# Moving the next head pair's query product to the end of two attention steps, and its cast on ScalarE behind another cast

## Chip, cores and metric

One Trainium2 chip, one of its cores. The metric is the device time of one execution in microseconds (us), lower is better. A profiled execution comes with its own time, its span (first to last instruction on the engines) and a trace of every instruction.

## What is computed

A block of three parts on x of shape 2 x 512 x 256 in float32: half a mixture-of-experts layer, causal attention with 16 heads of size 128 over a latent of size 64, and the same half layer again. Cut to what matters:

```python
x = x + 0.5 * ffn(layernorm(x))        # 12 experts, top 2, capacity 1.25
latents = x @ W_down.T                 # layernormed x; latent size 64
keys, values = latents @ W_uk.T, latents @ W_uv.T
q = x @ W_q.T                          # 16 heads of 128
scores = q @ keys.T / sqrt(128)        # causal, 512 x 512 for each head and sequence
x = x + (softmax(scores) @ values) @ W_o.T
x = x + 0.5 * ffn(layernorm(x))
```

## The kernel before

The weights of queries and keys are folded into one matrix (`Mq`), so that a head's queries live in the latent space and scores are products of queries (`uc`) with the latents (`latT_hi`, `latT_lo`). Values and output weights are folded in the same way (`Nv`), and are applied after the attention (line 1212). Every number is carried as a high and a low 16-bit part, so most products stand two or three times, and each result is read out of a PSUM bank twice: ScalarE (ACT) casts the high part, then VectorE (DVE) subtracts it and writes the low part.

The attention runs over 8 pairs of heads, `i`, and in each over 10 units of work, `j`; five units cover one head for both sequences. Each engine has its own program, in which `attention_step(i, j)` stands for j = 1 to 10 in a loop over the first 7 pairs (lines 1203, 585, 857) and once more, unrolled, for the last pair. Engines meet only at semaphores. In step j:

- TensorE (PE) makes the **scores** of unit j+4 (lines 1129 to 1131, the last one adds the mask), the **context** of unit j (lines 1152 to 1154) and the **transposes** of the probabilities of unit j+2 (line 1139). The context needs the low part of the transposed probabilities (`pTlo_ready`), the transposes need the exponentials.
- ACT makes the **exponentials** of unit j+3 (line 550) when their row maximum is there, and the **high part** of the transposed probabilities of unit j+2 (line 556).
- DVE makes the **low part** of unit j+1 (line 803), which needs ACT's high part, and the **row maximum** of unit j+4 (lines 794, 798), which needs the scores. In steps 3, 5, 8 and 10 it first copies a finished context out (lines 811, 812).
- GpSimd (POOL) divides the copied contexts (lines 415 to 421); the sync engine's queue (SP) moves queries and transposes contexts (lines 317, 309).

In steps 1 and 3 the **queries** of the next pair come in between, for the first and the second half of the tokens (`queries(i + 1, 0)`, `queries(i + 1, 1)`): PE makes them in six matmuls of 512 columns into bank 7 (line 900), ACT casts the high part (line 542), DVE subtracts (line 785), which is its last work in these steps, and SP then issues four transfers from `stage` to `uc` for each half (line 317). The scores of the next pair's unit 0 (made in step 6) wait for the first half's transfers, those of its unit 2 (made in step 8) for the second half's. Bank 7 also holds scores: those of unit 9, made in step 5, wait until both halves of the queries have been read.

Of the kernel before, what the change touches and what calls it, by code (L numbers as in the profile page):

```python
# [5 lines left out]
def bass_macaron_moe_mla_moe(  # L6
# [72 lines left out]
    with ctx:  # L79
# [196 lines left out]
        def tokens(t):  # L276
            return slice(t * HALF, (t + 1) * HALF)

        def blk(n):
            return slice(n * P, (n + 1) * P)  # L280

        def beyond(i, j):

            return isinstance(i, int) and i * UNITS + j >= NP * UNITS
# [146 lines left out]
        def _(act):  # L431
# [105 lines left out]
            def split_queries(i, t):  # L537

                if not isinstance(i, int):
                    act.wait_ge(u_moved[t], i * 64)  # L540
                act.wait_ge(u_ps, i * 2 + (t + 1))
                nc.scalar.copy(stage[:, 0, tokens(t)], bank[2 * t if isinstance(i, int) and i == 0 else 7][:, :]).then_inc(u_hi, 1)

            def exponent(i, j):

                u = j % UNITS
                act.wait_ge(max_ready, i * UNITS + (j + 1))
                for n, (b, q, at) in enumerate(HEAD_UNITS[u % HU]):
                    cols = slice(at, at + P * (q + 1))
                    last = nc.scalar.activation(prob[:, u % 2, cols], bank[SCORE_BANK[u]][:, cols], ACT.Exp,  # L550
                                                bias=nmax[:, u, n:n + 1])
                last.then_inc(prob_ready, 1)

            def split(i, j):
                act.wait_ge(pT_ps, i * UNITS + (j + 1))
                nc.scalar.copy(pT_hi[:, j % 2, :], bank[3 + j % 2][:, :]).then_inc(pThi_ready, 1)  # L556

            def attention_step(i, j, queries=True):
                if not beyond(i, j + 3):
                    exponent(i, j + 3)  # L560
                if queries and j in (1, 3):
                    split_queries(i + 1, j // 2)
                if not beyond(i, j + 2):
                    split(i, j + 2)

            split_N(0)
            for k in range(DC, 2 * DC):
# [14 lines left out]
            exponent(0, 2)  # L582
            split(0, 1)
            attention_step(0, 0)
            with act.Fori(0, NP - 1) as i:
                for j in range(1, UNITS + 1):
                    attention_step(i, j)
            for j in range(1, UNITS - 2):
                attention_step(NP - 1, j, queries=False)
# [16 lines left out]
        def _(dve):  # L606
# [181 lines left out]
            def row_max(i, j):  # L788
                u = j % UNITS
                dve.wait_ge(s_ps, i * UNITS + (j + 1))  # L790
                parts = HEAD_UNITS[u % HU]
                src = bank[SCORE_BANK[u]]
                if len({q for _, q, _ in parts}) == 1:
                    last = nc.vector.tensor_reduce(nmax[:, u, 0:len(parts)], src[:, :].rearrange("p (a n) -> p a n", a=len(parts)),  # L794
                                                   AX.X, ALU.max, negate=True)
                else:
                    for n, (b, q, at) in enumerate(parts):
                        last = nc.vector.tensor_reduce(nmax[:, u, n:n + 1], src[:, at:at + P * (q + 1)], AX.X, ALU.max, negate=True)  # L798
                last.then_inc(max_ready, 1)
# [93 lines left out]
        def _(pe):  # L893
            mm = nc.tensor.matmul

            def split_product(dst, left, right, K, start=True, stop=True):

                terms = [(0, 0, k) for k in range(K)] + [(0, 1, k) for k in range(K)] + [(1, 0, k) for k in range(K)]
                for n, (a, b, k) in enumerate(terms):
                    last = mm(dst, left(k)[a], right(k)[b], start=start and n == 0, stop=stop and n == len(terms) - 1)  # L900
                return last
# [201 lines left out]
            def queries(i, t):  # L1103

                first = isinstance(i, int) and i == 0
                if not first:
                    pe.wait_ge(u_lo, i * 2 + t)
                split_product(bank[2 * t if first else 7][:, :],
                              lambda k: [m[:, k, bass.ds(i * 2, 2), :].rearrange("p h l -> p (h l)") for m in Mq],
                              lambda k: [xT_hi[:, k, tokens(t)], xT_lo[:, k, tokens(t)]], DC).then_inc(u_ps, 1)  # L1110

            def scores(i, j):
                u = j % UNITS
                first_use = {0: 0, 2: 1}
                if u in first_use:
                    pe.wait_ge(u_moved[first_use[u]], i * 64 + 64 * (j // UNITS + 1))
                if HELD_BY[u] is None:
                    if not (isinstance(i, int) and i == NP - 1):
                        pe.wait_ge(u_lo, i * 2 + 4)
                else:  # L1120
                    held = HELD_BY[u] + j - u
                    if not (isinstance(i, int) and i * UNITS + held < 0):
                        pe.wait_ge(prob_ready, i * UNITS + (held + 1))
                dst = bank[SCORE_BANK[u]]
                for n, (b, q, at) in enumerate(HEAD_UNITS[u % HU]):
                    cols = slice(at, at + P * (q + 1))
                    keys = slice(SEQ * b, SEQ * b + P * (q + 1))
                    queries_of = uc[:, i * 2 + j // HU, SEQ * b + P * q:SEQ * b + P * (q + 1)]
                    mm(dst[:, cols], queries_of, latT_hi[:, keys], start=True, stop=False)  # L1129
                    mm(dst[:, cols], queries_of, latT_lo[:, keys], start=False, stop=False)  # L1130
                    last = mm(dst[:, cols][:, P * q:], identb[:, :], maskneg[:, :], start=False, stop=True)  # L1131
                last.then_inc(s_ps, 1)

            def transposes(i, j):
                pe.wait_ge(prob_ready, i * UNITS + (j + 1))
                if not (isinstance(i, int) and i == 0 and j < 2):
                    pe.wait_ge(pTlo_ready, i * UNITS + (j - 1))
                for k in range(SB):
                    last = nc.tensor.transpose(bank[3 + j % 2][:, blk(k)], prob[:, j % 2, blk(k)], ident[:, :])  # L1139
                last.then_inc(pT_ps, 1)  # L1140

            def context(i, j):
                unit = j % HU
                if unit == 0 or unit == 2:
                    pe.wait_ge(ctx_free, i * (2 * B) + (j // HU * B + unit // 2 + 1))
                pe.wait_ge(pTlo_ready, i * UNITS + (j + 1))
                for b, q, at in HEAD_UNITS[unit]:
                    dst = bank[5 + b][:, q * (LAT + 1):(q + 1) * (LAT + 1)]
                    for k in range(q + 1):
                        n = SB * b + k  # L1150
                        p_hi, p_lo = (p[:, j % 2, at + P * k:at + P * (k + 1)] for p in (pT_hi, pT_lo))
                        mm(dst, p_hi, lat[:, n, 0:LAT + 1], start=(k == 0), stop=False)  # L1152
                        mm(dst[:, 0:LAT], p_hi, lat[:, n, LAT + 1:2 * LAT + 1], start=False, stop=False)  # L1153
                        last = mm(dst, p_lo, lat[:, n, 0:LAT + 1], start=False, stop=(k == q))  # L1154
                if unit in LAST_UNIT:
                    last.then_inc(ctx_ps, 1)

            def attention_step(i, j, with_queries=True):
                if with_queries and j in (1, 3):
                    queries(i + 1, j // 2)  # L1160
                if not beyond(i, j + 4):
                    scores(i, j + 4)
                context(i, j)
                if not beyond(i, j + 2):
                    transposes(i, j + 2)

            pe.wait_ge(wuv_lo, 1)
            pe.wait_ge(woT_ready, 16 * 2 * DC)
# [31 lines left out]
            pe.wait_ge(lat_ready, 1)  # L1200
            pe.wait_ge(m_lo, 4)
            attention_step(0, 0)
            with pe.Fori(0, NP - 1) as i:
                for j in range(1, UNITS + 1):
                    attention_step(i, j)
# [11 lines left out]
            for j in range(1, UNITS):  # L1217
                attention_step(NP - 1, j, with_queries=False)
# [43 lines left out]
```

## Time and profile before

| what | value |
|---|---|
| median of 3 runs (lowest to highest) | 245.18 us (245.15 to 245.21) |
| profiled execution, its own time | 245.21 us |
| its span | 243.5 us |
| PE busy, share of the span | 231.6 us, 95% |
| DVE busy | 201.6 us, 83% |
| ACT busy | 163.2 us, 67% |
| POOL busy | 79.8 us, 33% |
| granted TensorE clock | 0.999 of full speed |

A row of a timeline gives a start, a duration, the engine, the line in the code and, in brackets, the idle time before it and what ended it. PE's matmuls are pipelined: the next one starts before the modelled end of the last, so the time that a part takes of PE is read from its start to the start of the next part. On DVE, too, an operation can start shortly before the row of the one ahead of it ends.

### The profile page before, as it was taken

To read this page: it belongs to the slowest core of one execution; us is meant where nothing else is said; L and a number is where in the kernel's file an instruction comes from. 1 tells how busy PE (TensorE), PEld (TensorE's weight loads), DVE (VectorE), ACT (ScalarE), POOL (GpSimd) and SP (SyncE) were. 2 spreads that over 40 slices of the span, in tenths; PEclk is the share of its full clock that TensorE was granted. 3 is DMA by queue.
4 is the path that set the end of the run, shared out by engine and by line. 5 is a ranking of instruction groups with operands and counts; after the bars stand their busy time and mean duration, and the time that the engine had idled before them with its cause. 6 is when DMAs were issued, how large, how long until landed. Compare 5 with 4: busy or idle time off the path is not lost.

```text
span 243.5 us, 7145 instructions
## 1 busy us (share of the span) xinstructions
PE 231.6 (95%) x2579; PEld 177.3 (73%) x2604; DVE 201.6 (83%) x480; ACT 163.2 (67%) x316; POOL 79.8 (33%) x135
## 2 busy tenths in 40 slices
PE   7699999899999999999999999999998899999995
PEld 2465479757777788787887787878886788865474
DVE  3978799987899999899999998999998338268793
ACT  2678883547788888879798888897988300344560
POOL 8351865000024344345234343452345000300320
PEclk9999999999999999999999999999999999999999
DMA  6999984002021025142160251331613310000005
GB/s 216 259 382 297 197 153 89 3 23 63 3 53 38 0 75 100 31 93 49 43 129 0 75 97 31 86 56 43 129 28 61 65 24 0 3 0 0 3 1 172
DMA packets 43128, 19.30 MB, mean 79 GB/s; under 512 B 33820, under 2 KB 42856, under 8 KB 42856
## 3 DMA queue, kind: packets, MB, share of 16 engines
q1 hardware_dynamic: 41912, 17.91, 32.0%
q10 hardware_dynamic: 1200, 1.18, 1.4%
q8 instruction: 10, 0.16, 0.3%
q14 instruction: 6, 0.05, 0.1%
HBM read 7.55 MB, written 1.05 MB: 35 GB/s over the span
## 4 chain that ended last, share of the span: by engine, by line
PE 75%; DVE 14%; DMA 4%; issue 3%; ACT 2%; SPq 1%; ACTq 0%; DVEq 0%
PE bank L949 12%; PE bank L1139 11%; PE bank L900 11%; PE bank L1212 9%; PE bank L1130 7%; PE bank L1129 4%; PE bank L1057 3%; PE bank L1153 3%; PE bank L1152 3%; PE bank L1154 3%; DMA cT<-in_L_ffn_w_dram 2%; DVE pT_lo L803 2%; PE bank L1131 2%; DVE nmax L794 2%; PE bank L907 2%
## 5 line engine op out<-in xcount | busy, mean ns | idle before, releaser
L550 ACT ACTIVATE prob<-bank,nmax 128x384 f32<-128x384 f32 (+3 forms) x128 | 62.2, 526 | 8.9 <-DVE nmax L794 7.4
L803 DVE TENSOR_TENSOR pT_lo<-bank,pT_hi 128x512 f16<-128x512 f32 x80 | 54.8, 685 | 3.0 <-ACT pT_hi L556 2.1
L556 ACT CAST pT_hi<-bank 128x512 f16<-128x512 f32 x80 | 46.7, 584 | 11.0 <-PE bank L1139 10.5
L1139 PE MATMUL bank<-ident,prob 128*128 128x128 f32 x320 | 50.5, 280 | 0.0
L415 POOL TENSOR_TENSOR cst<-craw,rsum 128x256 f32<-128x256 f32 x30 | 18.4, 612 | 87.0 <-DVE craw L812 87.0
L1152 PE MATMUL bank<-lat,pT_hi 128*128 128x65 bf16 x320 | 37.7, 193 | 1.9 <-DVE pT_lo L803 1.9
L1153 PE MATMUL bank<-lat,pT_hi 128*128 128x64 bf16 x320 | 37.8, 195 | 0.0
L1130 PE MATMUL bank<-latT_lo,wqo 128*128 128x384 bf16 (+3 forms) x128 | 36.6, 299 | 1.2
L1154 PE MATMUL bank<-lat,pT_lo 128*128 128x65 bf16 x320 | 37.5, 192 | 0.0
L1152 PEld LDWEIGHTS bank<-lat,pT_hi 128*128 128x128 f16 x320 | 30.1, 96 | 6.9 <-DVE pT_lo L803 2.0
L794 DVE TENSOR_REDUCE nmax<-bank 128x1 f32<-128x512 f32 (+1 forms) x48 | 32.8, 683 | 1.9 <-PE bank L1131 1.9
L1139 PEld LDWEIGHTS bank<-ident,prob 128*128 128x128 f32 x320 | 33.6, 140 | 0.0
L1154 PEld LDWEIGHTS bank<-lat,pT_lo 128*128 128x128 f16 x320 | 30.1, 99 | 0.0
L1153 PEld LDWEIGHTS bank<-lat,pT_hi 128*128 128x128 f16 x320 | 30.0, 97 | 0.0
L1129 PE MATMUL bank<-latT_hi,wqo 128*128 128x384 bf16 (+3 forms) x105 | 29.5, 282 | 0.4 <-DMA wqo<-stage 0.4
L1131 PE MATMUL bank<-maskneg,identb 128*128 128x128 bf16 x128 | 26.4, 219 | 0.0
L798 DVE TENSOR_REDUCE nmax<-bank 128x1 f32<-128x384 f32 x64 | 23.9, 416 | 2.0 <-PE bank L1131 2.0
L421 POOL TENSOR_TENSOR ffn_buf<-cst,woT_buf 128x256 f32 (+1 forms) x30 | 20.1, 671 | 4.8 <-POOL woT_buf L419 4.7
L1212 PE MATMUL bank<-Nv_hi,cT 128*128 128x256 bf16 x128 | 21.3, 273 | 0.0
L1212 PE MATMUL bank<-Nv_lo,cT 128*128 128x256 bf16 x64 | 17.4, 273 | 0.0
L1131 PEld LDWEIGHTS bank<-maskneg,identb 128*128 128x128 bf16 x128 | 12.5, 98 | 6.2
L1129 PEld LDWEIGHTS bank<-latT_hi,wqo 128*128 (+1 forms) x128 | 12.5, 98 | 4.6 <-issue 0.7
(168 smaller groups left out, 453.8 us busy)
## 6 DMA issues: line engine op xcount, KB each, us to landing
wqo<-stage SPq DMA_DIRECT2D x64, 64.0 KB, 2.0
wqo<-in_L_attn_W_o_dram SPq DMA_DIRECT2D x2, 1024.0 KB, 6.6
wqo<-in_L_attn_W_q_dram SPq DMA_DIRECT2D x1, 2048.0 KB, 14.3
out_dram<-X SPq DMA_DIRECT2D x8, 128.0 KB, 1.8
X<-in_L_attn_x_dram ACTq DMA_DIRECT2D x1, 512.0 KB, 7.1
cT<-in_L_attn_W_uk_dram SPq DMA_DIRECT2D x1, 512.0 KB, 16.1
cT<-in_L_attn_W_uv_dram SPq DMA_DIRECT2D x1, 512.0 KB, 11.6
cT<-in_L_ffn_w_dram SPq DMA_DIRECT2D x1, 384.0 KB, 4.9
```

The costliest lines, as they stand in the source:

```text
L550: last = nc.scalar.activation(prob[:, u % 2, cols], bank[SCORE_BANK[u]][:, cols], ACT.Exp, bias=nmax[:, u, n:n + 1])
L556: nc.scalar.copy(pT_hi[:, j % 2, :], bank[3 + j % 2][:, :]).then_inc(pThi_ready, 1)
L794: last = nc.vector.tensor_reduce(nmax[:, u, 0:len(parts)], src[:, :].rearrange("p (a n) -> p a n", a=len(parts)), AX.X, ALU.max, negate=True)
L803: nc.vector.tensor_tensor(pT_lo[:, j % 2, :], bank[3 + j % 2][:, :], pT_hi[:, j % 2, :], ALU.subtract).then_inc(pTlo_ready, 1)
L1129: mm(dst[:, cols], queries_of, latT_hi[:, keys], start=True, stop=False)
L1130: mm(dst[:, cols], queries_of, latT_lo[:, keys], start=False, stop=False)
L1131: last = mm(dst[:, cols][:, P * q:], identb[:, :], maskneg[:, :], start=False, stop=True)
L1139: last = nc.tensor.transpose(bank[3 + j % 2][:, blk(k)], prob[:, j % 2, blk(k)], ident[:, :])
L1152: mm(dst, p_hi, lat[:, n, 0:LAT + 1], start=(k == 0), stop=False)
L1153: mm(dst[:, 0:LAT], p_hi, lat[:, n, LAT + 1:2 * LAT + 1], start=False, stop=False)
L1154: last = mm(dst, p_lo, lat[:, n, 0:LAT + 1], start=False, stop=(k == q))
L1212: last = mm(bank[OUT_BANK[n]][:, 0:D], cT[:, i, part, n, :], Nv[w][:, i, :], start=(i == 0 and (part, w) == TERMS[0]), stop=(i == NP - 1 a ...
```

## The change

Two programs are reordered. On PE the queries of steps 1 and 3 move from the front of the step to its end, behind the transposes. On ACT the cast of the queries moves behind the high part of the transposed probabilities. Nothing is added or removed, and DVE, POOL and SP keep their order.

```diff
@@ ACT @@
             def attention_step(i, j, queries=True):
                 if not beyond(i, j + 3):
                     exponent(i, j + 3)
+                if not beyond(i, j + 2):
+                    split(i, j + 2)
                 if queries and j in (1, 3):
                     split_queries(i + 1, j // 2)
-                if not beyond(i, j + 2):
-                    split(i, j + 2)
@@ PE @@
             def attention_step(i, j, with_queries=True):
-                if with_queries and j in (1, 3):
-                    queries(i + 1, j // 2)
                 if not beyond(i, j + 4):
                     scores(i, j + 4)
                 context(i, j)
                 if not beyond(i, j + 2):
                     transposes(i, j + 2)
+                if with_queries and j in (1, 3):
+                    queries(i + 1, j // 2)
```

On PE, at the end of step 1 in the loop (1139 are the transposes, 900 the queries, 1129 to 1131 the scores of the next step), there stood before:

```order
 L1154 MATMUL bank<-lat,pT_lo 128x65
 L1135 REGISTER_ALU
 L1139 MATMUL bank<-ident,prob 128x128 x4
 L1129 ISA
 L1129 MATMUL bank<-latT_hi,wqo 128x512
 L1130 MATMUL bank<-latT_lo,wqo 128x512
 L1131 MATMUL bank<-maskneg,identb 128x128
```

and there stands now:

```order
 L1154 MATMUL bank<-lat,pT_lo 128x65
 L1135 REGISTER_ALU
 L1139 MATMUL bank<-ident,prob 128x128 x4
 L1107 ISA
 L900 ISA
 L900 MATMUL bank<-xT_hi,Mq_hi 128x512
 L900 ISA
 L900 MATMUL bank<-xT_hi,Mq_hi 128x512
 L900 MATMUL bank<-xT_lo,Mq_hi 128x512 x2
```

The six query matmuls, which stood ahead of step 1's scores, now stand between its transposes and the scores of step 2; step 3 changes in the same way.

On ACT, step 1 in the loop (550 is the exponential, 556 the high part of the transposed probabilities, 542 the cast of the queries):

```order
 L585 ISA
 L550 ACTIVATE prob<-bank0,nmax 128x512
+L555 REGISTER_ALU
+L556 CAST pT_hi<-bank4 128x512
 L540 ISA
 L541 ISA
 L542 CAST stage<-bank7 128x512
-L555 REGISTER_ALU
-L556 CAST pT_hi<-bank4 128x512
 L547 REGISTER_ALU
 L550 ACTIVATE prob<-bank1,nmax 128x384
```

The high part of unit 3 has moved ahead of the cast of the queries.

## Rows read from the trace of the kernel before

**Rows 1.** Busy time of each engine in the first and the seventh pair, from queries to queries.

```profile
core 0: us, PE busy (x) PEld busy (x) DVE busy (x) ACT busy (x) POOL busy (x), PEclk, DMA share, GB/s
64.20:81.03 16.83, 16.23 (x220) 13.07 (x221) 15.64 (x35) 14.12 (x30) 5.11 (x10) 1.00 0.14 34
162.21:178.44 16.23, 16.07 (x220) 13.22 (x222) 15.45 (x36) 13.84 (x29) 6.72 (x12) 1.00 0.30 65
```

**Rows 2.** Timeline of DVE in the seventh pair, steps 1 to 4 and the end.

```profile
162.15 0.68 DVE L803 TENSOR_TENSOR pT_lo<-bank,pT_hi 128x512 f16<-128x512 f32 x1
162.75 0.68 DVE L794 TENSOR_REDUCE nmax<-bank 128x1 f32<-128x512 f32 x1
164.27 0.76 DVE L798 TENSOR_REDUCE nmax<-bank 128x1 f32<-128x384 f32 x2 [0.25 <-PE bank L1131]
...
168.89 0.68 DVE L785 TENSOR_TENSOR stage<-bank,stage 128x512 bf16<-128x512 f32 x1
169.73 0.69 DVE L803 TENSOR_TENSOR pT_lo<-bank,pT_hi 128x512 f16<-128x512 f32 x1 [0.16 <-ACT pT_hi L556]
...
178.38 0.68 DVE L803 TENSOR_TENSOR pT_lo<-bank,pT_hi 128x512 f16<-128x512 f32 x1
```

**Rows 3.** Timeline of PE: queries and scores, then context, transposes and scores of the last pair.

```profile
113.54 0.60 PE L900 MATMUL bank<-xT_hi,Mq_hi 128*128 128x512 f16 x2
114.84 0.33 PE L1129 MATMUL bank<-latT_hi,wqo 128*128 128x384 bf16 x1
115.39 0.19 PE L1152 MATMUL bank<-lat,pT_hi 128*128 128x65 bf16 x1
...
167.53 0.27 PE L1129 MATMUL bank<-latT_hi,wqo 128*128 128x256 bf16 x1
...
179.12 0.20 PE L1152 MATMUL bank<-lat,pT_hi 128*128 128x65 bf16 x1
179.50 0.64 PE L1139 MATMUL bank<-ident,prob 128*128 128x128 f32 x4
179.97 0.38 PE L1129 MATMUL bank<-latT_hi,wqo 128*128 128x512 bf16 x1
180.46 0.19 PE L1152 MATMUL bank<-lat,pT_hi 128*128 128x65 bf16 x1
```

**Rows 4.** Timeline: a query product followed by PE's next scores, ACT's cast, DVE's subtraction.

```profile
118.84 0.27 PE L1129 MATMUL bank<-latT_hi,wqo 128*128 128x256 bf16 x1
119.05 0.58 ACT L542 CAST stage<-bank 128x512 bf16<-128x512 f32 x1
50.96 0.59 ACT L542 CAST stage<-bank 128x512 bf16<-128x512 f32 x1 [0.70 <-PE bank L900]
51.58 0.69 DVE L785 TENSOR_TENSOR stage<-bank,stage 128x512 bf16<-128x512 f32 x1
```

**Rows 5.** First pair: timeline and chain of waits; last line: all 64 transfers.

```profile
64.00 0.69 DVE L803 TENSOR_TENSOR pT_lo<-bank,pT_hi 128x512 f16<-128x512 f32 x1
70.86 0.69 DVE stage L785
73.35 3.44 DMA wqo<-stage
76.92 0.28 PE L1129 MATMUL bank<-latT_hi,wqo 128*128 128x256 bf16 x1 [0.45 <-DMA wqo<-stage]
DMA to landing us min/median/max: 1.9/2.0/3.4
```

**Rows 6.** Timeline of PE and DVE at the end of the attention, where PE waits.

```profile
185.34 0.68 DVE L803 TENSOR_TENSOR pT_lo<-bank,pT_hi 128x512 f16<-128x512 f32 x1
186.08 0.20 PE L1152 MATMUL bank<-lat,pT_hi 128*128 128x65 bf16 x1 [0.52 <-DVE pT_lo L803]
186.54 0.68 DVE L803 TENSOR_TENSOR pT_lo<-bank,pT_hi 128x512 f16<-128x512 f32 x1
187.37 0.19 PE L1152 MATMUL bank<-lat,pT_hi 128*128 128x65 bf16 x1 [0.28 <-DVE pT_lo L803]
```

## The prediction

> **What bounds the kernel now.** I read first the busy times cut by pair of heads [rows 1], because the change acts once in each of the 7 pairs of the loop. The reader is to see that a pair takes 16.23 us (the 7th stands there; the 5th and the 6th take the same), that PE is busy for 16.07 us of it, and that DVE is not far behind with 15.45 us. So PE sets the time, and DVE has only 16.23 - 15.45 = 0.78 us to lose in a pair.
>
> Then I read DVE in order of time [rows 2]. Operations of 512 columns that wait for nothing start 0.60 us apart (162.15, 162.75). DVE rests in steps 1 and 3 only, while PE is at the queries: 0.25 us before the row maximum in step 1, and 0.16 us, among others, behind the subtraction of step 3. From the low part at 169.73 to the end of the one at 178.38 + 0.68 = 179.06 it does not rest at all. In steps 4 to 10 the two engines run at nearly the same pace, and the queries are where DVE catches up.
>
> Last I read how the work is handed over. PE's parts [rows 3]: queries 114.84 - 113.54 = 1.30 us; scores 115.39 - 114.84 = 0.55 us (0.49 us with one piece of 512, 179.97 to 180.46); a context 179.50 - 179.12 = 0.38 us; transposes 179.97 - 179.50 = 0.47 us. ACT's cast of the queries can start 0.21 us after PE's next part (118.84, 119.05), takes 0.58 us, and DVE's subtraction follows 0.03 us later (51.58 against 50.96 + 0.59) [rows 4]. A context that waits starts 0.06 us after the end of its low part (185.34 + 0.68 = 186.02, 186.08) [rows 6].
>
> **The change, part by part.** No instruction is added, removed or made longer; waits move. Before, PE starts the queries at the front of step 1, while DVE still has the low part 1, a row maximum, the low part 2 and another row maximum ahead of it; when DVE comes to the subtraction, the cast is done. Now the queries stand behind context 1 and transposes 3, and context 1 itself waits for low part 1. DVE's program is unchanged, so the subtraction still stands ahead of low part 3, and whatever it waits for holds up low part 3, and so context 3.
>
> Count from the start of context 1, at 0. PE: context 0.38, transposes 0.47, queries 1.30, so 2.15. Cast: 2.15 + 0.21 = 2.36 to 2.94; subtraction at 2.97. DVE had finished low part 1 at -0.06, and the next three operations, 0.60 us apart and the last 0.76 long, end at about 1.82: it stands idle for 1.15 us. Low part 3 starts 0.60 us behind the subtraction and ends 0.69 later, at 4.26; context 3 can start at 4.32. PE, free since 2.15, has scores 6 (0.49), context 2 (0.38), transposes 4 (0.47) and scores 7 (0.55) to do, and is ready at 4.04: it waits 0.28 us. ACT's high part 3 starts when the transposes have landed, some 0.2 us into the queries, and takes 0.58 us of their 1.30, so it does not delay the cast behind it: that edit costs nothing. If it were not there, the cast of the queries would hold up high part 3, since the transposes now end first.
>
> Step 3 repeats this: from context 3 again 2.97 us to the second subtraction, at 7.29. DVE has a context copy more to do there and rests less. Behind the second subtraction DVE works without a gap: 0.60 us to low part 5, then 9.33 us (169.73 to 179.06) to the end of low part 11, which is the next pair's low part 1, and 0.06 us to its context [rows 2, 6]. That is 7.29 + 0.60 + 9.33 + 0.06 = **17.28 us**, and this chain closes on itself, so no pair behind another can be shorter. Does something else end later? PE alone needs from the end of the second queries (6.46) what it needs now from 167.53 to 178.44, where the pair ends, less step 3's own three parts: 10.91 - 1.40 = 9.51, and 0.55 for the scores ahead of the context: 16.5, or 16.7 with the 0.17 us for which scores 9 would wait for bank 7. Not longer. So the pair grows from 16.23 to 17.28 us, by 1.05 us, and DVE rests for 17.28 - 15.45 = 1.8 us of it in place of 0.78.
>
> The transfers are the one thing late next. Scores 12 in step 8 wait for the four transfers of the second half: the fourth is issued 73.35 - 70.86 = 2.49 us after the subtraction starts, lands 2.0 us later by the median, and the scores start 0.13 us behind (76.79, 76.92) [rows 5]. From there to the end of the pair are 81.03 - 76.92 = 4.11 us [rows 1, 5], and 0.55 for scores to the next context 1. In total 7.29 + 2.49 + 2.0 + 0.13 + 4.66 = 16.57 us, 0.71 us less than the chain through DVE: hidden. In the first pair that same transfer took 3.44 us, and PE waited for it [rows 5]. With 3.44 us the chain is 18.01 us and sets the first pair. I take the 3.44 us there, because it is the row of the very transfer concerned, and 2.0 us in the other six.
>
> On this the Trainium skill, "DMA: Bandwidth & Descriptors", section on the fixed cost of a transfer, has a rule: about 2.0 us plus the bytes at 436 GB/s. For the 64 KB here that is an estimate of 2.15 us, and with it the first pair would be 17.28 us too, and the time 251.8 us. The median of 2.0 us agrees with it, the first pair's 3.44 us does not.
>
> **The sum.** In the first pair, step 1 begins at 64.20, now with the queries; changed, with scores, and context 1 starts at 64.20 + 0.55 = 64.75 (low part 1 ends at 64.69) [rows 1, 5]. The next pair's comes 18.01 us later, at 82.76, and six more pairs of 17.28 us lead to 186.44. In the trace the last pair's context 1 starts at 179.12, and there too it has waited for its low part (179.06) [rows 2, 3]; no queries follow, so from there on all is as before. The attention ends 186.44 - 179.12 = 7.3 us later. The profiled execution took 245.21 us, 0.03 above the median of the runs, so the forecast is **252.5 us**, against 245.18. With 2.0 us for the transfer it is 251.8. If a waiting context starts 0.15 us behind its low part, as one does (187.22, 187.37) [rows 6], two such hand-overs in each of 7 pairs add 7 x 2 x 0.09 = 1.3 us: 253.8. If part of the chain overlaps better than I count, by 0.3 us in a pair, it is 2.1 us less, and 249.8 at the shorter transfer.
>
> **The rivals.** A difference under 0.2%, some 0.5 us, can hardly be told from no change here.
> - *DVE catches up* and only the 0.28 us at context 3 stay in each pair, 7 x 0.28 = 2 us: 247.2. For it: PE and DVE are nearly even. Against it: DVE has no gap from 169.73 to 179.06 in which to catch up, and its 15.45 us of work and 1.8 us of rest do not fit into 16.5. Chance 0.05.
> - *PE stays busy throughout*: if DVE enters step 1 early enough that context 1 need not wait, the stall falls into PE's own work: 245.2. Against it: low part 1 ends at 162.15 + 0.68 = 162.83, and without the queries ahead of it context 1 would be wanted at 162.22 + 0.55 = 162.77 [rows 1, 2]; DVE is late already. Chance 0.05.
> - *Faster*: a wait of PE goes. In step 8 of the first pair PE stands 0.45 us before scores 12 for the transfer of 3.44 us [rows 5], and that pair takes 16.83 us where a later one takes 16.23 [rows 1]. If the transfer is met at its usual 2.0 us, it lands 1.44 us sooner; so long as the second subtraction comes less than 1.44 us later against PE's own work, and PE's work covers every other wait, the 0.6 us are gain: 244.6. Against it: the later pairs would have to stall nowhere. Chance 0.04, half of it beyond 0.2%.
> - *The transfers set every pair*: if all of them take 3.44 us as in the first pair, 18.01 us in seven pairs, 6 x 0.73 = 4.4 us more: 256.9. Against it: the median over 64 is 2.0 us. Chance 0.03.
>
> **How the numbers follow.** The forecast has a chance of 0.83, and its own bounds, 249.8 to 253.8 with a little room above for hand-overs that I did not see, are the range: 249.8 to 254.1; the four rivals lie outside and hold 0.17. Slower: 0.83 + 0.05 + 0.03 = 0.91. Same: 0.05 and half of the third rival, 0.07. Faster: 0.02.
>
> **What would show it.** In the changed profile a pair (queries to queries) should take about 17.3 us from the second on; DVE should rest ahead of line 785, some 1.15 us in step 1 and less in step 3, released by ACT's line 542; PE should wait at line 1152 for DVE's line 803, at first by about 0.3 us; ACT's line 542 should wait for PE's line 900; PE's busy time should stay and DVE's too. The prediction is wrong if pairs still take 16.23 us, if DVE rests ahead of line 785 without PE waiting behind it, or if PE's waits end on transfers.

## The result, and the profile after

The changed kernel takes 252.07 us (median of 4, 252.02 to 252.4) against 245.17 us before (244.72 to 245.21): ratio 1.028, 95% interval 1.0258 to 1.0302. It is slower by 6.9 us; 252.5 was forecast. The profiled execution took 252.04 us with a span of 250.3, so the whole loss lies in the span (243.5 before).

The busy times by engine from the profile's page of the changed kernel: no engine has more work. DVE's 200.9 us were 201.6 before, ACT's 162.2 were 163.2. PE shows 235.7 in place of 231.6 with the same number of matmuls, and the groups of matmuls sum to the same (line 1139 to 50.5 us before and after, line 1130 to 36.6). What differs is when they start: the page counts time in which two matmuls overlap once, so matmuls that waits have pulled apart make more busy time.

```profile
PE 235.7 (94%) x2579; PEld 176.1 (70%) x2604; DVE 200.9 (80%) x480; ACT 162.2 (65%) x316; POOL 79.8 (32%) x135
```

The groups of instructions from the same page. The last column is the idle time ahead of a group:

```profile
L550 ACT ACTIVATE prob<-bank,nmax 128x384 f32<-128x384 f32 (+3 forms) x128 | 62.2, 526 | 17.4 <-DVE nmax L794 11.9
L556 ACT CAST pT_hi<-bank 128x512 f16<-128x512 f32 x80 | 46.6, 583 | 1.7 <-PE bank L1139 1.1
L785 DVE TENSOR_TENSOR stage<-bank,stage 128x512 bf16<-128x512 f32 x16 | 11.1, 692 | 14.6 <-ACT stage L542 14.6
```

Line 785, the subtraction of the queries, waited for the cast once before, for 0.7 us in the whole kernel; now DVE stands 14.6 us ahead of it. Cut by pair, from one first subtraction to the next, the first pair and two later ones (these answer to [rows 1]):

```profile
67.79:85.45 17.66, 16.70 (x223) 13.01 (x223) 15.35 (x35) 13.78 (x29) 6.72 (x12) 1.00 0.13 32
102.69:119.93 17.24, 16.66 (x223) 12.98 (x223) 15.26 (x35) 13.71 (x29) 6.72 (x12) 1.00 0.28 61
119.93:137.18 17.25, 16.67 (x223) 12.97 (x223) 15.26 (x35) 13.71 (x29) 6.72 (x12) 1.00 0.28 61
```

A pair takes 17.24 us in place of 16.23, with DVE working 15.26 us of it. The clock stays at 1.00. DVE in order of time in the seventh pair (answers to [rows 2]):

```profile
171.67 0.69 DVE L785 TENSOR_TENSOR stage<-bank,stage 128x512 bf16<-128x512 f32 x1 [1.16 <-ACT stage L542]
172.28 0.68 DVE L803 TENSOR_TENSOR pT_lo<-bank,pT_hi 128x512 f16<-128x512 f32 x1
...
175.98 0.69 DVE L785 TENSOR_TENSOR stage<-bank,stage 128x512 bf16<-128x512 f32 x1 [0.83 <-ACT stage L542]
176.59 0.68 DVE L803 TENSOR_TENSOR pT_lo<-bank,pT_hi 128x512 f16<-128x512 f32 x1
...
178.24 0.68 DVE L803 TENSOR_TENSOR pT_lo<-bank,pT_hi 128x512 f16<-128x512 f32 x1
...
185.22 0.68 DVE L803 TENSOR_TENSOR pT_lo<-bank,pT_hi 128x512 f16<-128x512 f32 x1
```

and PE beside it (answers to [rows 3]):

```profile
168.71 0.20 PE L1152 MATMUL bank<-lat,pT_hi 128*128 128x65 bf16 x1
...
172.68 0.22 PE L1131 MATMUL bank<-maskneg,identb 128*128 128x128 bf16 x1
173.02 0.20 PE L1152 MATMUL bank<-lat,pT_hi 128*128 128x65 bf16 x1
...
173.40 0.63 PE L1139 MATMUL bank<-ident,prob 128*128 128x128 f32 x4
173.87 0.59 PE L900 MATMUL bank<-xT_hi,Mq_hi 128*128 128x512 f16 x2
...
175.16 0.33 PE L1129 MATMUL bank<-latT_hi,wqo 128*128 128x384 bf16 x1
...
176.08 0.63 PE L1139 MATMUL bank<-ident,prob 128*128 128x128 f32 x4
177.03 0.38 PE L1130 MATMUL bank<-latT_lo,wqo 128*128 128x512 bf16 x1 [0.32 <-DVE stage L785]
...
178.74 0.22 PE L1131 MATMUL bank<-maskneg,identb 128*128 128x128 bf16 x1
178.99 0.20 PE L1152 MATMUL bank<-lat,pT_hi 128*128 128x65 bf16 x1
...
185.96 0.20 PE L1152 MATMUL bank<-lat,pT_hi 128*128 128x65 bf16 x1
```

DVE rests for 1.16 us, subtracts, and only then makes low part 3, which ends at 172.28 + 0.68 = 172.96; context 3 starts at 173.02, though PE was done with the mask of scores 7 some 0.06 us after 172.68 and so stood for about 0.28 us. Two places in this table need care. Where PE's wait is short, the page's column of idle time misses it, since the modelled end of a matmul covers it. And the first matmul of scores 9 (line 1129, some 0.21 us) has no record here: it started at about 176.81, and PE, free at 176.08 + 0.47 = 176.55, waited about 0.26 us for the second subtraction, not 0.32.

These are not PE's only waits. Context 6 starts at 178.99, 0.07 us behind the end of low part 6 (178.24 + 0.68 = 178.92), though PE was done with the mask ahead of it at about 178.80. Read in this way, from the starts of its rows, PE waits five times in a pair: about 0.28 us at context 3, 0.26 at scores 9, 0.10 at context 5, 0.19 at context 6 and 0.1 at context 1. Together they are 0.9 to 1.0 of the 1.02 us by which a pair is longer. In the kernel before, the same reading finds no wait of PE's from the fourth pair on.

### The profile page after: what moved, and what is told of

Its sections match the earlier page's. It is cut to its first block, busy times and chain, and to the rows that moved or that the text cites. A ratio compares the mean times of both kernels' runs of the same rounds, so it can differ in the third digit from the quotient of the medians.

```text
span 250.3 us, 7145 instructions
## 1 busy us (share of the span) xinstructions
PE 235.7 (94%) x2579; PEld 176.1 (70%) x2604; DVE 200.9 (80%) x480; ACT 162.2 (65%) x316; POOL 79.8 (32%) x135
## 4 chain that ended last, share of the span: by engine, by line
PE 69%; DVE 18%; issue 5%; ACT 3%; DMA 3%; SPq 1%; DVEq 1%
PE bank L949 12%; PE bank L900 10%; PE bank L1139 10%; PE bank L1212 8%; PE bank L1130 5%; DVE pT_lo L803 4%; PE bank L1152 4%; PE bank L1129 3%; PE bank L1057 3%; PE bank L1153 3%; PE bank L1154 3%; ACT stage L542 2%; DVE nmax L794 2%; PE bank L1131 2%; DVE xn L642 2%
## 5 line engine op out<-in xcount | busy, mean ns | idle before, releaser
L1139 PE MATMUL bank<-ident,prob 128*128 128x128 f32 x320 | 50.5, 280 | 0.0
L1130 PE MATMUL bank<-latT_lo,wqo 128*128 128x384 bf16 (+3 forms) x128 | 36.6, 299 | 3.1 <-DVE stage L785 2.3
L785 DVE TENSOR_TENSOR stage<-bank,stage 128x512 bf16<-128x512 f32 x16 | 11.1, 692 | 14.6 <-ACT stage L542 14.6
## 6 DMA issues: line engine op xcount, KB each, us to landing
cT<-in_L_attn_W_uk_dram SPq DMA_DIRECT2D x1, 512.0 KB, 16.2
```

## The experiments

The times of before beside them were 245.0 to 245.2 us. The length of a pair is read in each trace from one first subtraction to the next, from the third pair on.

**PE's half of the change alone.** ACT keeps the order of before.

```diff
 ACT: attention_step
+                if queries and j in (1, 3):
+                    split_queries(i + 1, j // 2)
                 if not beyond(i, j + 2):
                     split(i, j + 2)
-                if queries and j in (1, 3):
-                    split_queries(i + 1, j // 2)
```

> Only PE's half of the change: the queries stand at the end of steps 1 and 3, ACT casts them ahead of its high part as before. Theory (the subtraction on DVE holds up the low part behind it): 252.0 us, as with both halves. The cast takes ACT from 2.36 to 2.94 us behind the start of context 1, high part 3 then follows 0.50 us behind the cast's start, and ends at 3.44, before DVE can start low part 3 at 3.57; so ACT's order is worth nothing, and a pair still takes 17.24 us. Rival (ACT's order is what keeps the change from costing more, each high part 0.5 us later): 2 x 0.5 us more in each of 7 pairs, 259 us.

Measured: 252.14 us, ratio 1.0283 (1.0262 to 1.0303), a pair of 17.23 us. The order on ACT is worth nothing once PE's is changed; the whole loss is PE's half.

**ACT's half alone.** PE keeps the order of before, ACT casts the queries behind its high part (ACT's part of the change's diff).

> Only ACT's half: the queries stay at the front of steps 1 and 3 on PE, ACT casts them behind its high part. Theory: slower than the change itself, about 255 us. The cast now waits for the transposes at the end of the step, so the first subtraction ends some 4.7 us behind the start of the first queries, while PE wants the second queries (which reuse bank 7) at 4.0: 0.74 us; the second subtraction comes late in the same way, and scores 9, which also reuse bank 7, start 0.68 us late. Together 1.4 us in each of 7 pairs, a pair of 17.6 us; PE waits at the queries (line 900) and at the scores (lines 1129, 1130) for DVE's subtraction, and not at a context. Rival (ACT has slack, 13.8 us of 16.2 us busy in a pair, and its order does not matter): 245.2 us.

Measured: 257.63 us, ratio 1.0547 (1.0487 to 1.0607). The direction and the places are the theory's, the size is larger: a pair takes 18.03 us, 1.8 us more than before, where 1.4 were expected. PE's waits in one pair, where the queries and the scores wait for the subtraction, each with the transposes ahead of it:

```profile
122.30 0.63 PE L1139 MATMUL bank<-ident,prob 128*128 128x128 f32 x4
123.50 0.60 PE L900 MATMUL bank<-xT_hi,Mq_hi 128*128 128x512 f16 x2 [0.56 <-DVE stage L785]
...
127.10 0.63 PE L1139 MATMUL bank<-ident,prob 128*128 128x128 f32 x4
128.32 0.39 PE L1129 MATMUL bank<-latT_hi,wqo 128*128 128x512 bf16 x1 [0.59 <-DVE stage L785]
```

With 0.47 us for the transposes, the two waits are 123.50 - 122.77 = 0.73 us and 128.32 - 127.57 = 0.75 us, close to the 0.74 and 0.68 expected. What the theory had ruled out is a wait at a context: by the starts of PE's rows, contexts 5 and 6 wait 0.11 and 0.19 us behind the late second subtraction.

So a cast on ACT, which is busy for 13.8 us of the 16.2 of a pair, cost 12.6 us, more than the change itself, because it was made to wait for the transposes, and a PSUM bank that PE needs again waits for it. The two halves are not additive: PE's half takes the harm out of ACT's.

**Step 1 alone, and step 3 alone.** In each, one of the two query products moves on PE and ACT as in the change, the other keeps its place.

```diff
 PE: attention_step, step 1 alone (step 3 alone has 1 and 3 exchanged)
-                if with_queries and j in (1, 3):
+                if with_queries and j in (3,):
                     queries(i + 1, j // 2)
...
                     transposes(i, j + 2)
+                if with_queries and j in (1,):
+                    queries(i + 1, j // 2)
```

> The change in step 1 alone; in step 3 both engines keep the order of before. Theory (a chain from the low part through the queries to the next subtraction, which closes only when both steps are passed): far less than half of the loss. Context 3 now comes behind the second queries on PE, at 5.32 us behind the start of context 1, and its low part is ready at 4.26; DVE rests 1.15 us in step 1, but the way through DVE to the next context 1 is then about 16.4 us, against PE's 16.23: 245.2 to 246.6 us. Rival (each moved query product costs its own stall, half of the loss): 248.6 us.

> The change in step 3 alone; in step 1 both engines keep the order of before. Theory: from context 3 to the second subtraction 2.97 us, DVE then needs 9.93 us to the end of the next low part 1, which is 1.85 us after the next pair's first queries start and so hidden behind them; what is left is scores 9, which wait some 0.17 us for bank 7: a pair of 16.4 us, 246.4 us (245.2 to 246.8). Rival (each moved query product costs its own stall, half of the loss): 248.6 us.

Measured: step 1 alone 247.34 us, ratio 1.0096 (1.0075 to 1.0116), a pair of 16.59 us; step 3 alone 249.32 us, ratio 1.0177 (1.0156 to 1.0199), a pair of 16.80 us. Both expectations were too low, and the idea behind them fell: the two losses, 0.36 and 0.57 us in a pair, nearly add up to that of the change, 1.02. Nor is it half and half. Where the expectation for step 3 went wrong stands in its trace:

```profile
122.79 0.69 DVE L787 TENSOR_TENSOR stage<-bank,stage 128x512 bf16<-128x512 f32 x1 [1.13 <-ACT stage L542]
...
125.06 0.68 DVE L805 TENSOR_TENSOR pT_lo<-bank,pT_hi 128x512 f16<-128x512 f32 x1
```

```profile
124.59 0.63 PE L1141 MATMUL bank<-ident,prob 128*128 128x128 f32 x4
...
125.79 0.20 PE L1154 MATMUL bank<-lat,pT_hi 128*128 128x65 bf16 x1
```

(In this kernel line 787 is the subtraction, 805 the low part, 1141 the transposes, 1154 a context.) Between the late subtraction and low part 6 stand low part 5, a row maximum and a context copy; low part 6 ends at 125.74, and context 6 waits for it until 125.79, though PE could have begun at 124.59 + 0.47 + 0.55 = 125.61. I had followed the late subtraction to scores 9 only, and not two steps down DVE's queue. With scores 9, which wait 0.26 us where 0.17 were expected, and context 5, which waits 0.10, PE's waits come to 0.55 of the 0.57 us; they are the three that the changed kernel has behind its second subtraction. In step 1 alone, part of the loss is the second queries: they now come right behind step 2, and wait about 0.24 us for bank 7, which the late first subtraction still reads; I had left that wait out. Context 1, about 0.1 us late behind low part 1, is most of the rest.

**DVE's order changed as well.** The subtraction of the queries stands one step later, behind the low part that it held up.

```diff
 DVE: attention_step of the changed kernel
+                if queries and j in (2, 4):
+                    split_queries(i + 1, j // 2 - 1)
                 if not beyond(i, j + 4):
                     row_max(i, j + 4)
-                if queries and j in (1, 3):
-                    split_queries(i + 1, j // 2)
```

> The change as it is, and on DVE the subtraction of the queries one step later, behind the low part that it used to hold up and ahead of the row maximum. Theory (DVE's order makes the loss): nearly all of it comes back. Low part 3 ends some 2.4 us behind the start of context 1, where PE wants it at 4.04, so the contexts wait for nothing; the second subtraction starts at 7.0 us, and from there 9.33 us to the end of the next low part 1 and 0.06 to its context make 16.4 us for a pair, against 16.23 before: 246.4 us (245.2 to 247.2). Rival (PE's order itself costs the time, with the context ahead of the queries waiting for its low part whatever DVE does): 251 to 252 us.

Measured: 247.42 us, ratio 1.0091 (1.0064 to 1.0118). That lies above the range expected: two thirds of the loss come back, not nearly all, and a pair takes 16.53 us. PE's new order costs little by itself, DVE's queue made most of it a loss. What is left, 0.30 us in a pair, is nearly all one wait of PE's in each, about 0.27 us at scores 9 for the second subtraction (the first matmul of scores 9 has no record here either):

```profile
123.09 0.38 PE L1130 MATMUL bank<-latT_lo,wqo 128*128 128x512 bf16 x1 [0.33 <-DVE stage L785]
```

**Less work for PE, in the changed kernel and in the one before.** Six of the ten units leave out the product of queries with the low part of the latents, so the scores are less exact.

```diff
-                    mm(dst[:, cols], queries_of, latT_lo[:, keys], start=False, stop=False)
+                    if u not in (9, 0, 1, 2, 3, 4):
+                        mm(dst[:, cols], queries_of, latT_lo[:, keys], start=False, stop=False)
```

> The change as it is, with less work for PE: in six of the ten units (9, 0, 1, 2, 3, 4, made in steps 5 to 10) the scores leave out the product with the low part of the latents, which takes 0.21 to 0.22 us of PE in each, 1.3 us in a pair. Theory (the chain through DVE sets the pair): the pair stays at 17.2 us and the time near 252 us (251.3 to 252.3), PE only waits more. Rival (PE still sets the pair, its waits come on top): 7 x 1.3 us less, 243 us.

> The same six products left out of the kernel before. Theory (PE sets the pair there): a pair falls from 16.23 us until DVE sets it, whose work is 15.45 us: 239.5 to 241.5 us. Rival (DVE sets it there as well, and PE only looks busy): 245 us.

Measured: in the changed kernel 251.85 us (ratio 1.0272, 1.0238 to 1.0305), as the theory had it. In the kernel before 244.26 us (0.9961, 0.9941 to 0.9982): the theory fell there. The pair of the kernel before with 1.3 us less for PE, and of the changed kernel with the same:

```profile
132.11:148.33 16.22, 15.58 (x210) 12.26 (x212) 15.44 (x35) 13.74 (x28) 6.73 (x12) 1.00 0.30 65
```

```profile
119.54:136.78 17.24, 16.03 (x214) 12.08 (x214) 15.25 (x35) 13.64 (x29) 6.73 (x12) 1.00 0.28 61
```

16.22 us against 16.23 before the relief, and DVE rests in it as long as before. What PE was spared it waits: by the starts of its rows five contexts of a pair wait for low parts, 1.2 us together, of which the column of idle time shows two waits:

```profile
PE bank L1153 <- DVE pT_lo L803: 0.5, 2, 0.2
```

(Line 1153 is the context in this kernel; total, number and longest.) PE, busy for 99% of a pair before, was not what set it alone.

**Less work for DVE, with and without the relief of PE.** That raised the question whether DVE sets the pair of the kernel before. In units 4 to 9 the low part of the probabilities is written for half its columns only, and the context uses old values for the rest.

```diff
-                nc.vector.tensor_tensor(pT_lo[:, j % 2, :], bank[3 + j % 2][:, :], pT_hi[:, j % 2, :],
+                n = 256 if j % UNITS in (4, 5, 6, 7, 8, 9) else 512
+                nc.vector.tensor_tensor(pT_lo[:, j % 2, 0:n], bank[3 + j % 2][:, 0:n], pT_hi[:, j % 2, 0:n],
```

> The kernel before, with less work for DVE: in six of the ten units (4 to 9) the low part of the transposed probabilities is written for 256 of the 512 columns only, about 0.29 us less of DVE in each, 1.7 us in a pair. Theory (PE and DVE are equally long there, so that relief of either alone gives nothing, as relief of PE alone gave nothing): a pair stays at 16.2 us and the loop's share of the time does not move, 244 to 245.1 us, the last pair aside, which DVE sets alone and which may give up to 1 us. Rival (DVE alone sets the pair): 7 x 1.5 us less, 234 us.

> The kernel before with both reliefs: the six products of the scores left out on PE (1.3 us in a pair) and half the columns of six low parts left out on DVE (1.7 us in a pair). Theory (two chains of equal length): now a pair falls, to about 15.0 to 15.3 us, and the time to 236 to 239.5 us. Rival (something third sets the pair, ACT or the transfers): 244 to 245 us.

> The changed kernel with the same relief of DVE alone, half the columns of the low parts of units 4 to 9 left out. Theory (DVE's work between the second subtraction and the next context 1 is on the chain that sets the pair): the pair falls from 17.24 us until PE's own work behind the second queries sets it, at about 16.75 us, so 7 x 0.5 us less: 248.5 us (247.5 to 249.3). Rival (the loss comes from PE's new order, and relief of DVE does not help): 252 us.

Measured: the kernel before with less for DVE 243.51 us (0.9933, 0.9915 to 0.995), half a microsecond under the range expected; with less for both 238.12 us (0.9712, 0.9644 to 0.9781); the changed kernel with less for DVE 248.13 us (1.0121, 1.0049 to 1.0192). A pair of each, in this order:

```profile
131.97:148.17 16.20, 16.20 (x223) 13.12 (x221) 14.05 (x35) 13.89 (x28) 6.73 (x12) 1.00 0.30 65
```

```profile
113.55:128.91 15.36, 15.22 (x214) 12.30 (x212) 14.11 (x35) 13.55 (x28) 6.71 (x12) 1.00 0.32 68
```

```profile
118.64:135.42 16.78, 16.55 (x226) 13.04 (x223) 13.86 (x34) 13.87 (x29) 6.72 (x12) 1.00 0.29 63
```

In the kernel before, relief of PE alone leaves the pair at 16.22, of DVE alone at 16.20; of both, it falls to 15.36, just above the 15.0 to 15.3 expected. So two chains of the same length run there: PE's work, and DVE's work with its rests at the queries. The 1.7 us that relief of DVE alone saves do not come from the steady pairs: in the two profiled executions the five pairs behind the first are shorter by less than 0.2 us together. The first pair is shorter by 0.6 (16.22 us in place of 16.83), since PE no longer waits there for the late transfer, which I had not expected; and 1.0 us is saved behind the seventh pair's first subtraction, nearly all of it in the last pair, which has no queries for PE to spend time on. In the changed kernel DVE's chain is the longer one alone: relief of PE does nothing, relief of DVE takes the pair to 16.78, where 16.75 was expected from PE's own work behind the second queries. What is left over 16.23 are the two waits of PE's that this relief does not touch, 0.28 us at context 3 and 0.26 at scores 9.

**A try for a faster kernel.** In the kernel before, the second subtraction ahead of the row maximum for which DVE waits.

```diff
 DVE: attention_step of the kernel before
+                if queries and j == 3:
+                    split_queries(i + 1, j // 2)
                 if not beyond(i, j + 4):
                     row_max(i, j + 4)
-                if queries and j in (1, 3):
+                if queries and j == 1:
                     split_queries(i + 1, j // 2)
```

> The kernel before, with one operation moved on DVE: in step 3 the subtraction stands ahead of the row maximum of unit 7, for which DVE rests 0.27 us each time while the cast of the queries is already there. Theory: the second half's transfers start 0.55 us sooner in the first pair, so PE's 0.45 us wait there goes, and DVE enters the last pair 0.1 to 0.3 us earlier: 244.5 us (244.2 to 244.9). Rival (PE is busy throughout elsewhere, and the row maximum, 0.6 us later, holds up the exponential and with it PE's transposes of unit 7): 245.2 us or more.

Measured: 245.04 us against 245.08, ratio 0.9993 (0.9968 to 1.0017). The medians do not tell it from no change, and a pair still takes 16.22 us. In the profiled execution PE does not wait for the transfer in the first pair, but that was the fastest of the twelve (244.58 us), and runs of the kernel before reach 244.67. The premise was wrong as well: DVE now rests 0.33 us for the cast in step 3, where it rested 0.27 us for the scores, so the cast was not there yet. No kernel that computes the whole is shown to be faster than the one before.

## Why the prediction was right, point by point

**The chain.** It was forecast term by term from the start of context 1, and stands so in the trace of the seventh pair. From the rows of after: context 1 to the first subtraction, 171.67 - 168.71 = 2.96 us (forecast 2.97); subtraction to context 3, 173.02 - 171.67 = 1.35 us (forecast 4.32 - 2.97 = 1.35); context 3 to second subtraction, 175.98 - 173.02 = 2.96 (2.97); from there to low part 5, 0.61 (0.60); low part 5 to the end of low part 11, 185.90 - 176.59 = 9.31 (9.33); context 1 to context 1, 185.96 - 168.71 = 17.25 (17.28). A pair takes 17.24 us, 0.04 less than forecast. What DVE's trace of before shows without a gap [rows 2] it did again without a gap.

**The waits of PE** were forecast at context 3, 0.28 us, and are about 0.28; at scores 9, 0.17 us, and are about 0.26. The rest of the pair's 1.02 us, at contexts 5, 6 and 1, the prediction had in the length of the chain, but named no place for it. DVE rests 1.16 and 0.83 us ahead of line 785, 1.15 and "less" being forecast, and ACT's line 542 waits for PE's line 900 in all 14 cases of the loop. One sign failed: PE's busy time did not stay, it rose by 4.1 us on the page, with the same matmuls.

**ACT's edit costs nothing**: shown by PE's half alone, 252.14 against 252.07 us. That the cast would otherwise hold up high part 3 has no price in the time: in PE's half alone a pair takes 17.23 us, against 17.24. That ACT's edit is free holds only beside PE's edit; alone it is the costliest of all the orders tried.

**The first pair** is the mis-sized term: 18.01 us forecast, 17.66 between its first subtraction and the next. The fourth transfer of the second half took 3.11 us, not the 3.44 that I carried over [rows 5], and the chain runs through it, as forecast (the chain of waits of the changed kernel, then the scores that waited):

```profile
72.10 0.70 DVE stage L785
...
74.60 3.11 DMA wqo<-stage
```

```profile
77.85 0.28 PE L1129 MATMUL bank<-latT_hi,wqo 128*128 128x256 bf16 x1 [0.41 <-DMA wqo<-stage]
```

The next context 1 came at 82.50, where 82.76 was forecast; with six pairs 0.04 us shorter each, the last pair's came at 185.96, where 186.44 was forecast, and the median at 252.07, where 252.5 was. By the rule of the Trainium skill, "DMA: Bandwidth & Descriptors", on the fixed cost, an estimate of 2.15 us, the time would have been 251.8; that page of the Trainium skill fits the rule to transfers that GpSimd issues, and the sync engine issues these. The measured transfer of 3.11 us lies nearer to the row of before; as times, 251.8 and 252.5 are about equally far off, since the other pairs were each a little shorter than forecast.

**What was wrong in it** is the reading of the bound: "PE sets the time, and DVE has only 16.23 - 15.45 = 0.78 us to lose in a pair". DVE had nothing to lose. Its rests before are forced by the queries just as those after, and its work with them is as long as PE's (the two reliefs). The sum did not suffer, since it was made on the chain and not on the 0.78 us. But the wrong reading came back in the experiments: it made me expect that one moved step would find cover, and that less work for PE would shorten the kernel before.

**The rivals.** *DVE catches up*: no; in steps 4 to 10 it has no gap. *PE stays busy throughout*: no; it waits five times in a pair. *Faster*: no; the transfer of the first pair took 0.33 us less, but was issued later, at 74.60 us in place of 73.35, and PE still waited for it, 0.41 us by the column of idle time. *The transfers set every pair*: no; PE waits for a transfer once in the attention, and the median stays at 2.0 us.

## What to carry to other kernels

Work moved on the engine that is busiest has its price on the engine that takes the result: if that one works in order and its next instruction is one that others wait for, a wait that it did not have before goes down its whole queue, so follow it until the slack is used up and not only to the first instruction behind it. An engine that rests for 0.78 us in 16.23 has no 0.78 us to give as long as the rests are themselves handed over by a loop; relieve each engine alone and then both, to see which chains are of one length. And where two engines' orders belong together, change and measure each half alone: ACT's half was free here beside PE's, and alone it made the slowest kernel of all that were tried.

## What the runs showed of the hardware

Two things were not expected. The last transfers of the first pair, and no others, land late: 3.44 us before, 3.11 after, 3.18 and 3.24 in PE's half and in step 1 alone, against a median of 2.0. The traces show something that goes with it. The DMA engines also load instructions (the queues marked `instruction` in the view of DMA), and at this point of each of the 13 kernels there is a load of 16 KB: in the kernel before from 73.91 us for 1.54 us, in the changed one from 74.48 us for 1.43 us. Every transfer of queries that took more than 2.2 us, in any of the 13, was under way during that load, and at no other point did a transfer of queries meet a load of that size. That the load is the cause was not tried.

And an engine can be busy for 16.07 of 16.23 us in a loop and be spared 1.3 us of work (six products of 0.21 to 0.22 us) without the loop getting shorter: 16.22 us.
